# GpSimd's LayerNorm operations in four parts beside named rows of VectorE, in a graph kernel on one core

## The reference, cut to what matters

```
A = sigmoid(U @ U.T)                 # the same for all batches
K = 0.5 * (W + W^T) * A
d = rsqrt(max(K.sum(-1), 1e-12))
y = w_scale * (K * d[:,None] * d[None,:]) @ x
out = layernorm(x + y)               # over the 64 channels, no affine part
```

## Time and profile before

| | |
|---|---|
| median of 3 runs | 559.32 us (559.29 to 559.76) |
| span of the profiled execution | 557.6 us |
| TensorE matmul busy | 530.7 us, 95% |
| VectorE busy | 433.7 us, 78% |
| ScalarE busy | 217.9 us, 39% |
| GpSimd busy | 99.3 us, 18% |
| HBM read and written | 138.54 MB, 4.19 MB |
| mean granted TensorE clock | 0.994 |

### The profile page before, as it was taken

How to read it: one execution, slowest core, us unless ns; L and a number is a source line. 1 busy time by engine, 2 the same in 40 slices (tenths; PEclk the granted TensorE clock), 3 DMA queues, 4 the chain that set the end, 5 groups by cost and what they waited for, 6 DMA issues and landing times.

```text
span 557.6 us, 9999 instructions
## 1 busy us (share of the span) xinstructions
PE 530.7 (95%) x3208; PEld 296.0 (53%) x3208; DVE 433.7 (78%) x1113; ACT 217.9 (39%) x654; POOL 99.3 (18%) x61
## 2 busy tenths in 40 slices
PE   4899999999999999999999999999999999999991
PEld 4685445654556545555456544665456554564430
DVE  5898566875999659985799759997599956997554
ACT  2894413532245414344145332444134531444311
POOL 0000010001150013300214011410133002130153
PEclk9999999999999999999999999999999999999997
DMA  8997899758977699578985879776996688945003
GB/s 272 387 332 274 292 341 300 248 207 297 338 250 244 215 352 316 211 201 291 356 280 209 269 275 352 226 260 201 356 319 240 188 299 320 321 171 168 1 0 75
DMA packets 102850, 142.98 MB, mean 256 GB/s; under 512 B 37296, under 2 KB 37296, under 8 KB 102832
## 3 DMA queue, kind: packets, MB, share of 16 engines
q1 hardware_dynamic: 88240, 139.08, 71.7%
q10 hardware_dynamic: 14592, 3.67, 3.6%
HBM read 138.54 MB, written 4.19 MB: 256 GB/s over the span
## 4 chain that ended last, share of the span: by engine, by line
PE 80%; DVE 8%; issue 6%; ACT 3%; POOL 1%; DMA 1%; POOLq 0%; DVEq 0%
PE yp L309 39%; PE kt L294 21%; PE tw L280 17%; DVE k L481 3%; DVE k L491 2%; ACT k L410 1%; ACT gate L401 1%; PE yp L342 1%; DMA h<-in_L_gnn_U_dram 1%; PE tw L332 1%; DVE h L528 1%; DVE z L511 1%; PE tw L374 0%; POOL h L222 0%; PE yp L374 0%
## 5 line engine op out<-in xcount | busy, mean ns | idle before, releaser
L410 ACT ACTIVATE k<-kt 128x512 f32<-128x512 f32 (+3 forms) x288 | 151.7, 528 | 297.5 <-PE kt L294 292.6
L309 PE MATMUL yp<-k,z 128*64 128x512 f32 x960 | 247.5, 612 | 2.8 <-DVE z L511 2.8
L481 DVE TENSOR_TENSOR k<-tw,k 128x512 f32<-128x512 f32 (+2 forms) x320 | 193.4, 606 | 33.8 <-PE tw L280 30.5
L491 DVE CUSTOM_DVE_ANT_0 k<-k,gate 128x512 f32<-128x512 f32 (+2 forms) x320 | 217.2, 681 | 0.3 <-ACT gate L401 0.3
L294 PEld LDWEIGHTS kt<-ident,k 128*128 128x128 f32 x960 | 106.2, 140 | 128.7 <-ACT k L410 90.3
L280 PE MATMUL tw<-ident,k 128*128 128x128 f32 x1088 | 169.5, 275 | 2.7 <-DVE k L481 1.2
L294 PE MATMUL kt<-ident,k 128*128 128x128 f32 x960 | 157.8, 282 | 1.7 <-ACT k L410 1.7
L280 PEld LDWEIGHTS tw<-ident,k 128*128 128x128 f32 x1088 | 126.1, 140 | 30.5 <-issue 13.2
L309 PEld LDWEIGHTS yp<-k,z 128*64 128x64 f32 x960 | 52.1, 135 | 64.2 <-issue 58.6
L239 POOL TENSOR_TENSOR d<-deg,minus_half 128x4 f32<-128x4 f32 (+1 forms) x24 | 29.2, 1217 | 316.8 <-DVE deg L501 316.8
L410 ACT ACTIVATION_READ_ACCUMULATOR k<-kt 128x1 f32 x288 | 57.1, 198 | 0.0
(11 more groups left out here) (60 smaller groups left out, 116.3 us busy)
## 6 DMA issues: line engine op xcount, KB each, us to landing
k<-in_adj_dram SPq DMA_DIRECT2D x128, 1024.0 KB, 7.2
xt<-in_x_dram ACTq DMA_DIRECT2D x7, 512.0 KB, 7.0
out_dram<-h SPq DMA_DIRECT2D x7, 512.0 KB, 8.7
xt<-in_x_dram SPq DMA_DIRECT2D x1, 512.0 KB, 14.1
out_dram<-k SPq DMA_DIRECT2D x2, 256.0 KB, 2.6
h<-in_L_gnn_U_dram SPq DMA_DIRECT2D x1, 128.0 KB, 4.3
ws<-in_L_gnn_w_scale_dram ACTq DMA_DIRECT2D x1, 0.5 KB, 2.9
```

What stands on the lines that cost most here:

```text
L309: t = pe.matmul(yp[at:at + C, m // 2, :], z[:, n * G + c, :], K[(n, m)][:, c, :], start=(q == first_unit[m] and c == 0), stop=(q == last_u ...
L410: nc.scalar.activation(K[(j, i)][:, r, c0:UW], kt[:, g % RING, 0:UW - c0], ACT.Copy, accum_out=deg_parts[:, n, part:part + 1]).then_inc(up ...
L481: nc.vector.tensor_tensor(row, tw[:, tw_bank(g), 0:w], row, ALU.add).then_inc(sum_done, 1)
L491: nc.vector.tensor_tensor_reduce(row, row, A[:, A_AT[g]:A_AT[g] + w], 1.0, 0.0, ALU.mult, ALU.add, deg_parts[:, i * G + r, j:j + 1]).then_ ...
```

## The change

The add, the centring and the division of the six loop turns are each four operations of 256 columns, and each part first waits for `lower_done` of a named row of VectorE: 12 to 15 for the add, 17 to 20 for the centring, 27 to 30 for the division. The add's first two parts wait for the first half of `scale_y` alone. The places on the other engines move: `KEEP_AT` 6 to 12, `MEAN_AT` 11 to 16, `SQUARE_AT` 13 to 22, `VAR_AT` 15 to 22. On GpSimd the power for `rstd` and the power of the first degree group now stand ahead of the division. Semaphores count four for each batch where they counted one. After the loop the parts are not paced.

```diff
-Y_AT, KEEP_AT, MEAN_AT, SQUARE_AT, VAR_AT, COPY_AT = 5, 6, 11, 13, 15, 26
+Y_AT, KEEP_AT, MEAN_AT, SQUARE_AT, VAR_AT, COPY_AT = 5, 12, 16, 22, 22, 26
+LN_PARTS = 4
+ADD_ROWS, CENTER_ROWS, DIVIDE_ROWS = [12, 13, 14, 15], [17, 18, 19, 20], [27, 28, 29, 30]
...
             def store(b):
-                sp.wait_ge(normed, b + 1)
+                sp.wait_ge(normed, LN_PARTS * (b + 1))
...
-            def add_x(b):
-                pool.wait_ge(y_scaled, 2 * b + 2)
+            def part(k):
+                return slice(k * NC // LN_PARTS, (k + 1) * NC // LN_PARTS)
+
+            def beside_row(b, row):
+
+                pool.wait_ge(lower_done, b * NL + row)
+
+            def add_x(b, paced):
                 pool.wait_ge(x_kept, b + 1)
-                nc.gpsimd.tensor_tensor(h[:, :, :], h[:, :, :], x_keep[:, :, :], ALU.add).then_inc(h_ready, 1)
-
-            def center(b):
+                for k in range(LN_PARTS):
+                    pool.wait_ge(y_scaled, 2 * b + (2 * k // LN_PARTS + 1))
+                    if paced:
+                        beside_row(b + 2, ADD_ROWS[k])
+                    nc.gpsimd.tensor_tensor(h[:, part(k), :], h[:, part(k), :], x_keep[:, part(k), :],
+                                            ALU.add).then_inc(h_ready, 1)
...
-            def divide(b):
+            def spread(b):
                 pool.wait_ge(var_ready, b + 1)
                 nc.gpsimd.tensor_tensor(rstd[:, :], var[:, :], minus_half[:, :], ALU.pow).then_inc(rstd_ready, 1)
+
+            def divide(b, paced):
                 pool.wait_ge(rstd_ready, b + 1)
-                nc.gpsimd.tensor_tensor(h[:, :, :], h[:, :, :], per_row(rstd, 0, NC),
-                                        ALU.mult).then_inc(normed, 1)
+                for k in range(LN_PARTS):
+                    if paced:
+                        beside_row(b + 2, DIVIDE_ROWS[k])
+                    nc.gpsimd.tensor_tensor(h[:, part(k), :], h[:, part(k), :],
+                                            per_row(rstd, part(k).start, part(k).stop),
+                                            ALU.mult).then_inc(normed, 1)
...
             with pool.Fori(2, B) as b:
-                finish(b - 2)
-                for k in range(NZ):
+                add_x(b - 2, True)
+                center(b - 2, True)
+                spread(b - 2)
+                degrees(b, 0)
+                divide(b - 2, True)
+                for k in range(1, NZ):
                     degrees(b, k)
...
             def square(b):
-                act.wait_ge(centered, b + 1)
+                act.wait_ge(centered, LN_PARTS * (b + 1))
...
                 if not early:
-                    act.wait_ge(h_ready, b)
+                    act.wait_ge(h_ready, LN_PARTS * b)
...
             def row_mean(b):
-                dve.wait_ge(h_ready, b + 1)
+                dve.wait_ge(h_ready, LN_PARTS * (b + 1))
```

More of the change, by code:

```diff
@@ L204, in _ @@
             for k in range(2):
-                sp.wait_ge(normed, B - 1 + (k + 1))
+                sp.wait_ge(normed, LN_PARTS * (B - 1) + (k + 1))
                 sp.dma_start(rows_of(out, B - 1)[:, 8 * k:8 * k + 8, :], h_last(k)).then_inc(h_moved, 16)
@@ L217, in _ @@
             pool.wait_ge(const_ready, 2)
-            def add_x(b):
-                pool.wait_ge(y_scaled, 2 * b + 2)
-                pool.wait_ge(x_kept, b + 1)
-                nc.gpsimd.tensor_tensor(h[:, :, :], h[:, :, :], x_keep[:, :, :], ALU.add).then_inc(h_ready, 1)
-            def center(b):
-                pool.wait_ge(mean_ready, b + 1)
-                nc.gpsimd.tensor_tensor(h[:, :, :], h[:, :, :], per_row(mean, 0, NC),
-                                        ALU.add).then_inc(centered, 1)
@@ L230, in divide, with center @@
+            def center(b, paced):
+                pool.wait_ge(mean_ready, b + 1)
+                for k in range(LN_PARTS):
+                    if paced:
+                        beside_row(b + 2, CENTER_ROWS[k])
+                    nc.gpsimd.tensor_tensor(h[:, part(k), :], h[:, part(k), :],
+                                            per_row(mean, part(k).start, part(k).stop),
+                                            ALU.add).then_inc(centered, 1)
+            def spread(b):
                 pool.wait_ge(var_ready, b + 1)
@@ L239, in degrees @@
                 nc.gpsimd.tensor_tensor(d[:, s], deg[:, s], minus_half[:, s], ALU.pow).then_inc(d_ready, 1)
[L241 to L244, removed]
             for b in range(2):
@@ L249, in _ @@
             with pool.Fori(2, B) as b:
-                finish(b - 2)
-                for k in range(NZ):
-                    degrees(b, k)
-            finish(B - 2)
-            pool.wait_ge(normed, B - 1)
+                add_x(b - 2, True)
[4 more added lines that the diff above has]
+                for k in range(1, NZ):
+                    degrees(b, k)
+            add_x(B - 2, False)
+            center(B - 2, False)
+            spread(B - 2)
+            divide(B - 2, False)
+            pool.wait_ge(normed, LN_PARTS * (B - 1))
             for k in range(2):
@@ L467, in _ @@
                 nc.scalar.activation(K[(0, 0)][:, k, :], yp[:, k, :], ACT.Copy).then_inc(y_copied, 1)
-                act.wait_ge(centered, B - 1 + (k + 1))
+                act.wait_ge(centered, LN_PARTS * (B - 1) + (k + 1))
                 nc.scalar.activation(K[(0, 1)][:, k, :], K[(1, 0)][:, k, :], ACT.Square).then_inc(squared, 1)
@@ L581, in finish_last @@
                 nc.vector.tensor_tensor(hk, hk, xt[:, s, :], ALU.add).then_inc(h_ready, 1)
-                dve.wait_ge(h_ready, done)
+                dve.wait_ge(h_ready, LN_PARTS * (B - 1) + (k + 1))
                 if k == 0:
-                    dve.wait_ge(centered, B - 1)
+                    dve.wait_ge(centered, LN_PARTS * (B - 1))
                 nc.vector.tensor_reduce(mean[:, s], hk, AX_X, ALU.add).then_inc(h_summed, 1)
```

## The result

The changed kernel takes 597.22 us (median of 4 runs, 595.82 to 598.90) against 559.31 (558.80 to 559.76): 1.0676 times as long, 95% interval 1.0655 to 1.0698. Forecast were 585.7 and a range up to 591. The direction was right, 37.9 us slower, and the size was not.

What follows compares the result with a forecast made beforehand. TensorE bounds the kernel, busy 64.68 of 65.45 us a turn. A turn loses 3.05 + 1.2 = 4.25, six turns 25.5, tail 0.9: +26.4, so 585.7 us; range 575 to 591 for 8 in 10.

Steps and rivals of the forecast that it cites:

- The stall before `kt` of row 16: TensorE waits there for ScalarE, whose x_keep waits for the fourth add part: 3.74 us a turn.
- what the locks gave back: TensorE's waits at row 10's transpose and `kt` of row 14 vanish: 0.30 + 0.44 = 0.74 us a turn.
- the price of that stall: Before `kt` of row 16: 3.74 us plus 0.05 refilling the pipeline; less the 0.74 gained, 3.05 a turn.
- The second loss: Square and variance both due at row 22 make the products of row 28 start 1.2 us later a turn.
- Prices of a part: GpSimd's 256-column parts: 0.73 us for add, 0.62 for centre and divide; gate products 0.14 or 0.03 late.
- The gain: Shorter GpSimd operations remove TensorE's first two losses, at rows 10 and 14: 0.74 us a turn.
- Store and x load: SyncE's store of `h` and the x load, some 10 us later, cost nothing.
- The tail: After the loop, unpaced parts of centre and divide cost 0.9 us in all.
- A (gain): Rival: stall at row 16, square and variance are hidden; only the 0.74 gain remains, 555.8 us; 5 in 100.
- D (powers lock too): Rival: GpSimd's powers also lock VectorE's gate product, 2.3 us later a turn, 600 us; 3 in 100.
- B: Rival: only the first stall; VectorE makes up its 1.2 us before row 28's products, 578.5 us; 15 in 100.
- C, no change: Rival: the stall at row 16 only equals what the locks gave back, within 1 us in all; 2 in 100.

Runs made afterwards that it cites:

- both moves: The changed kernel with x_keep at row 16 instead of 12 and the square at row 21 instead of 22: 555.80 us, 0.9925 of the kernel before.
- the extra copies: The kernel before, whole unpaced GpSimd operations, with x_keep at row 12 and made five more times there: 598.96 us, 1.0700 of before.

## Why the prediction was right in kind and wrong in size

- **The stall before `kt` of row 16** was forecast in place, releaser and size: 3.74 us, measured 5.89 − 2.25 = 3.64. Less what the locks gave back it was 3.05 a turn, measured 2.85. Moving one ScalarE step removes it, moving the add's rows scales it. Shown.
- **The step that failed is the price of that stall.** The prediction says "Stall 3.74, and 0.05 for refilling the pipeline", and took every operation behind it at its duration from before. The operations behind it ran at a lower granted clock, 1.64 us a turn more, 9.8 us in six turns. The measured 597.2 less this is 587.4, inside the range. The upper end of 591 was built from the prices of the parts and a microsecond or two for pauses between engines; a resource that had stood at 1.00 for the whole loop was not among the unknowns, though the change put into each turn an idle time of TensorE longer than any in the loop before (0.37). The Trainium skill ("TensorE: Matmul & The Clock Gate", Part 1: The HAM clock gate) says that the gate lets TensorE's clock fall from 2.4 to 1.2 GHz when it idles and raises it again with activity; by that rule the stall can cost twice, and the traces agree: 1.00 without it, 0.50 behind it. The runs add that it is not sure: the same 3.47 us went without loss in two of the turns with the square at row 21 and in one with the copy of y at row 25. Nor is its size fixed. What decides it in a given turn stays open.
- **The second loss**, square and variance both at row 22: forecast 1.2, measured 1.58. The variance's wait, the `rstd` power just clearing the power for `d`, and z came as worked out (z ended 1.09 later than before, relative to `tw` of row 22). I left out two things that hang on the same late product. `kt` of row 26 is the first of its step and waits for `lower_done` of row 23: 1.23 us of idle. And ScalarE's copy of y stands behind that upper row, and was the last thing that the products waited for. The experiments with the square at row 21 and the copy at row 25 show both.
- **Prices of a part**: 0.73 and 0.62 forecast, 0.73 and 0.61 measured. They were the middles of ranges of 0.28 and 0.27 us, with no row behind the middle, so that they came out to 0.01 was luck. Gate products 0.14 late beside an add part, measured 0.16; 0.03 beside the others, measured 0.04.
- **The gain**, 0.74 a turn, is real: 0.78 with both moves in. That it comes from the shorter locks alone is argued, not shown.
- **Store and x load** cost nothing, as said: the store is issued at 331.87, ahead of the next load at 332.89.
- **The tail**: 0.9 forecast, 0.6 measured.
- The sum by terms: 26.4 forecast; 9.8 for the clock, 2.3 for the second loss, less 1.2 for the first and 0.3 for the tail, make 37.0, against spans that differ by 37.1.
- **The rivals.** A (gain) is what the kernel does once the two moves are mended, and not before. D (powers lock too) is refuted again: 0.68 beside the 2.91 us power. B is refuted: the second loss was larger, not gone. C, no change, is refuted by the 37.9 us.

## What to carry to other kernels

When an operation is moved later in one engine's program order, look at everything that stands behind it there, and ask which engine further on needs that within its ring of buffers: here a copy of 1 us, put in front of an upper row, cost 5.3 us a turn. A stall on TensorE costs its length, and it can cost once more in what follows it at the lower clock (up to 2.9 us here); price both, and give the range the second as an unknown where idle times are short now. Where an operation of one engine holds up another engine's, try splitting it before pacing it: here the parts alone brought the longest gate product from 2.55 to 1.07 us, and the waits that pin the parts to rows added 0.33 us a turn, each of them a new chain through other engines.

## What the runs showed of the hardware that I had not expected

- TensorE's granted clock fell to 0.50, its lower level, while it worked behind an idle time of 3.47 us in the turns that were hit, and behind 2.11 us in two turns of six; behind 0.57 us it never did. The loss was 1.6 us a turn in the changed kernel, 1.4 to 1.6 with the square at row 21, and up to 2.9 with the copy of y at row 25 and with the extra copies. Whether a given stall is followed by it differed among turns that were otherwise alike.
- The lock between VectorE's two-operand product and GpSimd works both ways, and the other engine gets its turn between two instructions: four 256-column parts back to back took 3.76 us beside gate products and 2.78 without them, and no product took over 1.07 us, where one whole 1024-column operation made it 2.55.
- A power of 16 columns on GpSimd holds it for 2.91 us without lengthening a gate product beside it (0.68).
